# Decoder layer: score and maximum products of the cross attention on row halves, query split and key rotation moved to the queries stage

## What is computed

```python
q = rope(norm(x1) @ Wq per head, absorbed by w_kc_q)          # 16 heads x 192
q = q @ W_qr @ W_kr                                           # 16 heads x 64 per row
k = rope(ctx)                                                 # 1444 x 64
p = softmax(q @ k.T)                                          # 1600 query rows x 1444 keys per item
x2 = x1 + (p @ k) @ w_kc_kv @ Wo
```

## Time and profile before

| | |
|---|---|
| median of 3 runs | 2810.13 us (2808.91 to 2810.47) |
| profiled execution, its own time | 2809.89 us |
| its span, first to last instruction | 2807.7 us |
| mean granted TensorE clock | 0.971 of 2.4 GHz |
| PE busy over the span | 2641.3 us (94%) |
| DVE, POOL, ACT busy | 1903.4, 1643.6, 1152.6 us |
| maxima on DVE (L1543) | 1248 reads, 784.6 us |
| additions on POOL (L1434) | 352, 1312.2 us |

### The profile page before, as it was taken

The page is one execution under the profiler, slowest core; times in us unless marked ns, Lnnn a source line. Parts: engine busy times, 40 slices in busy tenths (PEclk is TensorE's granted clock), DMA queues, the critical chain, the costliest instruction groups (busy, mean ns, idle before and its releaser), DMA issues. The chain is left out here.

```text
span 2807.7 us, 41100 instructions
## 1 busy us (share of the span) xinstructions
PE 2641.3 (94%) x13650; PEld 1637.2 (58%) x13650; DVE 1903.4 (68%) x3015; ACT 1152.6 (41%) x1793; POOL 1643.6 (59%) x566
## 2 busy tenths in 40 slices
PE   6999769999979999999999999999999999999598
PEld 4545467777635555555555555555555555555388
DVE  6888755545377776777677767776777777774575
ACT  3323235555424444444444444444444444444143
POOL 1544513434417776777677767776777677767321
PEclk9999879999969999999999999999999999999799
DMA  4000032121210011001100110001101110100011
GB/s 120 19 18 23 12 110 48 41 52 42 58 31 20 21 26 35 20 20 25 35 20 20 25 32 23 20 25 31 24 20 25 27 28 20 25 18 3 25 42 41
DMA packets 56341, 89.07 MB, mean 32 GB/s; under 512 B 7163, under 2 KB 47311, under 8 KB 56161
## 3 DMA queue, kind: packets, MB, share of 16 engines
q1 hardware_dynamic: 56288, 88.40, 12.5%
HBM read 65.24 MB, written 23.14 MB: 31 GB/s over the span
## 5 line engine op out<-in xcount | busy, mean ns | idle before, releaser
L1434 POOL TENSOR_TENSOR x_acc<-x_acc,x_prob 120x1600 f32<-120x1600 f32 (+1 forms) x320 | 1156.9, 3615 | 282.6 <-ACT x_prob L1450 278.8
L1543 DVE TENSOR_REDUCE x_mx<-x_ring 124x1 f32<-124x480 f32 (+3 forms) x1248 | 784.6, 658 | 425.1 <-PE x_ring L1653 424.5
L1450 ACT ACTIVATE x_prob<-x_scores 120x800 f32<-120x800 f32 (+1 forms) x768 | 633.8, 840 | 919.4 <-PE x_scores L1600 912.7
L1612 PE MATMUL x_context<-x_prob,x_kv 120*64 120x400 f32 (+1 forms) x3072 | 654.1, 519 | 0.0
L1597 PE MATMUL x_scores<-x_qa,x_ka 128*120 128x400 f32 (+1 forms) x1536 | 551.5, 359 | 0.0
L1600 PE MATMUL x_scores<-x_qb,x_kb 128*120 128x400 f32 (+1 forms) x1536 | 530.3, 345 | 0.0
L1653 PE MATMUL x_ring<-x_ka,x_qa 128*124 128x480 f32 (+3 forms) x1248 | 516.8, 437 | 3.1 <-DVE x_mx L1543 1.1
L1653 PEld LDWEIGHTS x_ring<-x_ka,x_qa 128*124 128x124 f32 (+1 forms) x1248 | 220.0, 186 | 321.9 <-issue 161.8
L1597 PEld LDWEIGHTS x_scores<-x_qa,x_ka 128*120 128x120 f32 (+1 forms) x1536 | 279.7, 182 | 107.3 <-issue 60.6
L1434 POOL TENSOR_TENSOR x_acc<-x_prob 121x1600 f32<-121x1600 f32 x32 | 155.3, 4853 | 248.8 <-ACT x_prob L1450 248.8
L1612 PEld LDWEIGHTS x_context<-x_prob,x_kv 120*64 120x64 f32 (+1 forms) x3072 | 167.0, 135 | 227.6 <-issue 162.9
(11 more groups left out here) (167 smaller groups left out, 2928.5 us busy)
## 6 DMA issues: line engine op xcount, KB each, us to landing
x_qraw<-scratch_qp SPq DMA_DIRECT2D x64, 400.0 KB, 5.1
scratch_qp<-q_qs SPq DMA_DIRECT2D x32, 400.0 KB, 3.7
x_raw<-in_ctx SPq DMA_DIRECT2D x32, 360.0 KB
a_x<-in_x SPq DMA_DIRECT2D x8, 400.0 KB
scratch_x<-a_x SPq DMA_DIRECT2D x8, 400.0 KB
q_x<-scratch_x SPq DMA_DIRECT2D x8, 400.0 KB
x_xr<-scratch_x SPq DMA_DIRECT2D x32, 100.0 KB
scratch_x<-x_x SPq DMA_DIRECT2D x32, 100.0 KB
```

The lines of the kernel that those rows point to most:

```text
L1434: pool.tensor_tensor(acc[0:rows, parity], first, prob[0:rows, c % PR], ALU.add).then_inc(acc_done.sem, 1)
L1450: act.activation(prob[0:rows, c % PR, u * HALF:(u + 1) * HALF].rearrange("p (j s) -> p j s", j=2), psc[0:rows, u, :, 0:BANK], ACT.Exp).the ...
L1543: dve.tensor_reduce(mx[0:block_rows(r), r, i:i + 1], ring[0:block_rows(r), bank, 0:b - a], AX.X, ALU.max).then_inc(rg.read[bank], 1)
L1612: mm = pe.matmul(pav[DC * s:DC * s + DC, j, 0:BANK], kv[0:rows, parity, c], prob[0:rows, c % PR, cols], start=c == 0, stop=c == LC - 1)
```

## The change

- **Scores.** The contraction is 64 deep, so it now stands on one half of the rows: queries of quarter j = 0 on rows 0 to 63, those of j = 1 on rows 64 to 127. Keys stand on both. For each half u there are three pairs of products (high·high, low·high, high·low). The two of a pair use different rows and different PSUM banks.
- **Key steps.** Scores are not made anew in each step. PSUM keeps them, and step c adds the product with the difference of its keys to those of step c-1. So the row of negated maxima is added in step 0 alone, as a fourth pair (`onerow`, `mq`). The differences are split into `dh` (ACT) and `dl` (DVE) behind transposes `dT`.
- **Maxima.** 7 row blocks of 115 queries for each row half, times three spans: 21 pairs of products of the high parts alone (`qm`, `kh`), that is 42 DVE reads. They stand in steps 1 to 10. `kh` comes from three more transposes `kT`.
- **Order.** A step is scores 0, a pair of maxima, scores 1, the other pairs, context. `den` moves from step 10 to steps 4 and 5 and is copied by ACT; its reciprocal is made in halves in steps 6 to 9, and `normalise` stands in steps 10 and 11. `mT` moves to step 11.
- **Queries stage.** The split of the queries (ACT high, DVE low), the rotation of the keys (POOL) and their differences (DVE) are made here; SP loads the context and stores `qh`, `ql`, `kr`, `kd`. POOL waits there for the weights of the cross stage, which hold the key tables.
- **Loads of the cross stage.** `kr` and `kd` twice each (once per row half, in pieces of 64 values), `kv` from `kr`, `qm`, `qh`, `ql` in halves.

The diff, cut to its core:

```diff
 queries stage
+            def store_k(k, i):
+                sp.wait_ge(k_diffed.sem, k_diffed.at(k, i + 1))
...
             def slot(k, parity, more):
...
+                for i in range(GB):
+                    if i + 2 < GB or not is_at(k, NG - 1):
+                        load_k(k, i + 2)
+                    if i == GB - 1 and more:
+                        load(k + 2, parity)
+                    store_k(k, i)
+                    if i < GB - 1:
+                        store(k, i)
...
+            def rope_products(k, i):
...
+                pool.tensor_tensor(kt1[:], kraw[:, i % 2], cosk[:], ALU.mult).then_inc(k_terms.sem, 1)
+                for to, frm in ((slice(0, half), slice(half, DC)), (slice(half, DC), slice(0, half))):
+                    pool.tensor_tensor(kt2[:, :, to], kraw[:, i % 2, :, frm], sink[:, :, to],
+                                       ALU.mult).then_inc(k_terms.sem, 1)
...
+                    if p % 2 == 0:
+                        rope_products(k, p // 2)
+                    else:
+                        rope_sum(k, p // 2)
...
+            ahead[0].wait(pool)
...
-                for side in range(2):
-                    cp = act.copy(qs[:, buf, :, 2 * (p % 2) + side],
-                                  pp[DC * side:DC * side + DC, p % 2, 0:GT].rearrange("e (b s) -> e b s", b=GB))
+                act.copy(qsh[:, buf, :, p % 2], pp[:, p % 2, 0:GT].rearrange("e (b s) -> e b s", b=GB)
+                         ).then_inc(p_high.sem, 1)
...
+                dve.tensor_tensor(qsl[:, buf, :, p % 2], pp[:, p % 2, 0:GT].rearrange("e (b s) -> e b s", b=GB),
+                                  qsh[:, buf, :, p % 2].bitcast(F32), ALU.subtract).then_inc(p_copied.sem, 1)
...
+                dve.tensor_tensor(kdiff[:], krot[:, i % 2, 1:LC], krot[:, i % 2, 0:LC - 1],
+                                  ALU.subtract).then_inc(k_diffed.sem, 1)
 cross stage
+        pairs = iter([[("max", t, r, i) for t in range(2)] for r in range(MB) for i in range(3)])
+        order = []
+        for c in range(LC):
+            if c == 0:
+                order.append([("kT", 2), ("out",), ("context",), ("scores", 0), ("scores", 1), ("dT", 0), ("dT", 1)])
+                continue
+            count = 0 if c == LC - 1 else 3 if c == 1 else 2
+            own = [("scores", 0)]
+            own += next(pairs) if count > 0 else []
+            own += [("scores", 1)]
+            own += [u for _ in range(count - 1) for u in next(pairs)]
+            own += [("dT", 2)] if c == 1 else [("mT",), ("kT", 0), ("kT", 1)] if c == LC - 1 else []
+            own += [("context",)]
+            own += [("den", c - 4)] if c in (4, 5) else []
+            order.append(own)
...
+            def scores(n, parity, c, u):
                 rows, a = rows_of(c), start_of(c)
+                cols = slice(u * BANK, (u + 1) * BANK)
+                halves = [slice(DC * j, DC * j + DC) for j in range(2)]
+                pe.wait_ge(exp_done.sem, exp_done.at(n, 2 * c + u - 1))
...
+                for k, q in ((dh, qh), (dl, qh), (dh, ql)):
+                    last = c > 0 and q is ql
+                    for j, part in enumerate(halves):
+                        mm = pe.matmul(psc[0:rows, u, j, 0:BANK], k[part, parity, a:a + rows], q[part, parity, cols],
+                                       start=c == 0 and k is dh and q is qh, stop=last,
+                                       skip_group_check=c > 0)
+                if c == 0:
+                    if u == 0:
+                        pe.wait_ge(m_loaded.sems[parity], m_loaded.done(n, parity))
+                    for j, part in enumerate(halves):
+                        mm = pe.matmul(psc[0:rows, u, j, 0:BANK], onerow[part, 0:rows], mq[part, parity, cols],
+                                       start=False, stop=True)
...
+                    a, b = span[i]
+                    part = slice(DC * t, DC * t + DC)
+                    mm = pe.matmul(ring[0:block_rows(r), bank, 0:b - a], qm[part, r * MR:r * MR + block_rows(r)],
+                                   kh[part, a:b], start=True, stop=True)
...
+            def copy_steps(n, parity, i):
...
+                act.copy(dh[:, parity, a:b], ring[:, bank, 0:b - a]).then_inc(dh_copied.sem, 1)
...
+            def low_steps(n, parity, i):
...
+                dve.tensor_tensor(dl[:, parity, a:b], ring[:, bank, 0:b - a], dh[:, parity, a:b].bitcast(F32),
+                                  ALU.subtract).then_inc(rg.read[bank], 1)
...
+                    if c in (6, 7, 8, 9):
+                        invert(n, (c - 6) // 2, (c - 6) % 2)
+                    if c >= LC - 2:
+                        normalise(n, c - (LC - 2))
```

More of the change, by code:

```diff
@@ new lines, in phase_cross_attention, with made, made_at @@
+        assert next(pairs, None) is None
+        is_unit = lambda u: u[0] not in ("scores", "context")
+        beside = [[u for u in own if is_unit(u)] for own in order]
+        units = [u for own in beside for u in own]
+        def made(n, u):
+            if u[0] == "kT":
+                return n + (2 if u[1] < 2 else 1) <= B - 1
+            return n <= B - 2 or u[0] in ("out", "den")
+        def made_at(n, u):
+            return made(n, u) if isinstance(n, int) else True
+        ends = [(n,) + u for n in (B - 2, B - 1) for u in units if made(n, u)]
@@ new lines, in load_half, with load_qm @@
+            def load_half(t, name, n, j):
+                src = d[name][bass.ds(n, 1), :, :, j].rearrange("b e u n -> (b e) u n")
+                return sp.dma_start(t[DC * j:DC * j + DC].rearrange("e (u n) -> e u n", u=2).bitcast(F32), src)
+            def load_qm(n):
+                if not is_at(n, 0):
+                    bank, value = rg.place(n - 2, ("max", 1, MB - 1, 2))
+                    wait(sp, rg.filled[bank], value)
+                for j in range(2):
+                    load_half(qm, "qh", n, j).then_inc(qm_loaded.sem, 16)
@@ L1441, in _ @@
             act.sem_inc(exp_done.sem, exp_done.credit)
+            for bank in range(2):
+                act.sem_inc(rg.read[bank], rg.credit)
             def exponentials(n, c, u):
@@ L1518, in normalise, with invert @@
+            def invert(n, j, half):
+                bank, value = rg.place(n, ("den", j))
+                dve.wait_ge(rg.read[bank], value)
+                cols = slice(half * (BANK // 2), (half + 1) * (BANK // 2))
+                dve.reciprocal(rden[:, j, cols], dens[:, j, cols]).then_inc(rden_ready.sem, 1)
             def normalise(n, j):
-                bank, value = rg.place(n, ("den", j))
+                wait(dve, ctx_saved.sem, ctx_saved.at(n, 0))
+                dve.wait_ge(rden_ready.sem, rden_ready.at(n, 2 * j + 2))
+                bank, value = rg.place(n, ("out",))
@@ L1574, in _ @@
             for j in range(2):
+                for half in range(2):
+                    invert(B, j, half)
                 normalise(B, j)
@@ L1614, in context @@
[L1614 to L1624 removed]
+                    pe.wait_ge(kv_loaded.sems[parity], kv_loaded.done(n, parity))
@@ L1672, in _ @@
+            for i in range(2):
+                make(-2, 0, ("kT", i))
             in_turn(pe, slot)
-            for j in range(2):
-                context(B - 1, 1, LC - 1, j)
-            for u in ends:
+            context(B - 1, 1, LC - 1)
+            for u in (("out",), ("den", 0), ("den", 1)):
                 make(B, 0, u)
```

522 lines of the change are left out of this document (288 added, 234 removed).

## The result

The changed kernel takes 2966.97 us (median of 4 runs, 2965.83 to 2971.38) against 2810.07 (4 runs): the ratio is 1.056, 95% interval 1.054 to 1.058. It is slower by 157 us, 5.6%. The profiled execution's span is 2965.2 us. First the page of the kernel after: busy time, granted clock by slices, the DMA, and two groups (busy us, mean ns, idle time before them).

What follows compares the result with a forecast made beforehand. PE was taken to bound the kernel, with the changed cross stage waiting for DVE's reads of the maxima. 2809.9 us plus 132 (31 items), 5 (queries stage) and 1 (before the first item) gave 2948 us, range 2790 to 3080.

Steps and rivals of the forecast that it cites:

- (A): The forecast itself: 2948 us for the whole kernel, own range 2890 to 3060, chance 0.57.
- rival C: Clock falls to the 1.2 GHz level in key step 1: about +2.5 us per item, 3026 us; chance 0.14.
- The ring's wait: Key steps 2 to 10: second pair of maxima waits for both DVE reads of the first; 4.36 us a step, 3.22 without waits.
- 0.12 shorter: Range case in the cross stage: release of a bank 0.12 us shorter at 13 places, -48 us.
- Score pairs at 0.18: Cross stage scores: the two products of a row-half pair overlap fully, 0.18 us per pair; 0.36 without overlap.
- rival D: Second pair of maxima finds its banks free, PE never held by the ring: item 46.9 us, whole 2525 us; chance 0.15.
- B's sum: Rival in which score pairs do not overlap: +7.7 us per item, 3187 us; chance 0.05.
- Step 1: Cross stage key step with three pairs of maxima behind transposes in the same banks: 7.5 us, its products sum to 4.0.
- Step 0 and step 11: First and last key steps of a cross stage item: priced at 8.3 and 4.0 us.
- The queries stage: Stage ahead of the cross stage: PE stays the bound, POOL and DVE have room; sum +5 us, 0 to 20.
- My sign for a stage over 377 us: A queries stage longer than 377 us would show POOL as its new bound.
- Before the first item: Maxima ahead of the first item +2.2, rotation and query split about -5, transposes and copies +4: +1 us, -4 to +6.

## Why the prediction was right, and where its sum was off

The forecast (A) was 2948 us, the result 2967. The sign and the main mechanism were right. That the item came out within 0.2 us was luck: at the full clock it is 1.2 us shorter than forecast, and a fall of the clock that the forecast had left to rival C put 1.0 of it back. The terms:

- **The ring's wait.** Forecast 4.36 a step, measured 4.23. From context to the next first pair it is 2.13 us, forecast 2.14; from first pair to context 2.10, forecast 2.22. Nearly the whole difference is in the release of a bank, the "0.12 shorter" of my range: I had put a weight load of 0.18 us between the end of a read and the product, and in the records product and load start together, 0.06 us behind the read; the context behind them comes 0.40 us later for my 0.31. That the wait, not PE's work, makes the step is shown by the halved reads (3.73) and the two other orders (3.7).
- **Score pairs at 0.18.** Right: measured 0.18, and 0.36 with one row half. My estimate by the weight loads (0.20, from the Trainium skill, TensorE: Matmul & The Clock Gate, LDWEIGHTS) does not show here: the two loads of a pair start within 0.01 us of each other, and I had put them one after the other. The factor of two of the Trainium skill (TensorEngine Tiling (Array Packing), Theoretical Speedup) holds for the products, but not for the kernel: rival D needed free banks besides. B's sum as I wrote it gives 7.55 us an item, not 7.7, and leaves out scores 0 of step 11; with them it is 8.1, which is what the one-half kernel measured.
- **Step 1.** Forecast 7.5, measured 7.06 at full clock and 8.70 where the clock falls. So rival C came true in two of three items, as an addition, at 1.6 us instead of my 2.5.
- **Step 0 and step 11.** 8.14 for 8.3 and 4.69 (1451.79 to 1456.48) for 4.0; in step 11 0.68 is the wait for the maxima's row behind `normalise`, which I hadn't seen. An item at full clock takes 59.39, the mean is 60.39, the forecast 60.6: errors of both signs met.
- **The items together.** +119.4 for +132: 60.39 for 60.6 gives 6.5 of it, and the mean item before was 56.54, not 56.34 (its first distance was 62.6), which gives the other 6.
- **The queries stage.** The step that failed. I priced POOL's rotation and DVE's subtractions by their lengths alone, said "both have room there", and gave +5, 0 to 20; it was +26. POOL's load was near (307.4 of 357 us; I had 41.3 of 44.6 a group, 330 of 357). What I did not price is that DVE's difference can't run beside POOL's products. With turns the stage ends 4.5 us later than before, near the +5 of the forecast, though its terms aren't shown one by one (the first rotation starts 1.2 us later, where I had put 3 for the wait and the first key rotation). My sign for a stage over 377 us, that POOL is the new bound, would have misled: the stage took 383, and POOL's load did not set it. The rows had the effect in them: the 4.93 us of the earlier trace rows, which I took for a slower rate of POOL, is an addition held by DVE's split. And `normalise` took 1.70 us in the mean in the kernel before (L1528, 56 in the middle of the cross stage), three times its 0.57 alone.
- **Before the first item.** +11 (37 less 26) for my +1. From the last absorb's end to the first maximum it is 24.5 us before and 25.2 after; from there to the first scores 33.8 and 48.1; from the scores to POOL's first addition 10.6 and 6.5. The middle part holds 21 pairs at 1.50 (I said 1.51) and both sums `den`, as before, but now also four halves of reciprocals that each delay a pair by 0.9 us, twelve transposes of keys, 2.5 us, and an output product of 5.4 us (granted clock 0.67) ahead of the scores. I had counted maxima and transposes and not what the slot's new order puts between them.

## What to carry over

When a product gets cheaper by packing, look first at who empties its bank: two banks filled by one pair serve only if other work as long as both reads stands behind each pair. Here one other order of the key step gave back 148 of the 157 us that the whole change had lost. Before an elementwise operation is given to VectorE or GpSimd, look whether both then work on SBUF operands at the same time: one of them stands, and what is queued behind it stands too. Making the engines take turns was worth 22.6 us here; giving both operations to one engine was worth 105 us where steps were short and 9 where they weren't.

## What the runs showed of the hardware

VectorE's operation on two SBUF operands did not run beside GpSimd's: whichever came first, the other stood. In the queries stage seven of 32 such operations stood behind five of GpSimd's in a row (6.35 to 6.39 us for 0.88; 5.6 us for one element per partition), 22 got in behind the first (1.3 to 1.7 us), and then GpSimd's next operation stood (mostly a rotation, 1.69 us for 1.04). What decides between the two isn't shown: 22 got in although GpSimd had another rotation to make. VectorE's operations that read PSUM were not held (maxima of 0.65 us and rotations of 0.56 to 0.57, with GpSimd at work and without). The Trainium skill (SBUF — State Buffer, SBUF: two separate sides) tells of a port pair that the two share and that one instruction locks for its whole length; the traces agree, except that seven times the lock went past VectorE several times in a row. In the cross stage, where each addition waits for a semaphore, VectorE got in between two of them.

Six products on two row halves took 0.65 us in either order of the program. By the records' names, products that stand three places apart in the program started within 0.02 us of each other in nearly all cases; so where the text on the kernel before calls each queue strictly in program order, these records don't bear it out for TensorE's products.
